# Expert attention of a gated mixture layer: four score slots and a two-tile delay, carried across query blocks, in place of two slots and a one-tile delay

## The chip, the cores and the metric

The kernel runs on all 8 cores of one Trainium2 chip. Each core works on its own batch element and shares nothing with the others but the chip. The metric is device time in microseconds (us) of the slowest core, for one launch.

## What is computed

For each batch element (4096 rows of 1024 values) the reference normalizes the rows, runs a 16-head attention `s`, runs a routed single-head attention `ffn` with 8 experts, and returns `x + s * silu(ffn)`. The change touches only the single-head attention inside `ffn`:

```python
q = jnp.einsum('tc,ecd,te->td', x, q_proj, m)      # D = 128, m is the routing mask
k = jnp.einsum('tc,ecd,te->td', x, k_proj, m)
v = jnp.einsum('tc,ecd,te->td', x, v_proj, m)
scores = jnp.einsum('bqd,bkd->bqk', qh, kh) / jnp.sqrt(D)
scores = jnp.where(causal, scores, jnp.finfo(scores.dtype).min)
attn = jax.nn.softmax(scores, axis=-1)
attn_out = jnp.einsum('bqk,bkd->bqd', attn, vh).reshape(b * t, D)
final = jnp.einsum('td,edc,te->tc', attn_out, o_proj, m * routing_weights)
```

## The kernel before

The kernel is written out by hand: every engine has its own program, and semaphores join them. It runs in stages. First the rows are normalized and transposed and the routing logits computed (up to about 220 us of the span). Then q, k and v of the routed attention are projected, 32 row tiles long (to 568 us). Then comes the stage that the change touches, the causal attention with one head of width 128, from 568.3 to about 710 us. After it the output projection with its Silu writes `g_sp` (to about 895 us), and the 16-head attention and the final combination take the rest, about 2,650 us.

The touched stage works on 8 query blocks `j` of 512 queries. Block `j` sees T = 4j + 4 key tiles `t` of 128 keys, 144 tiles in all; the running number of a tile is g = `c2_g(j, t)`. For every tile four engines take part:

- TensorE computes the scores of 128 keys by 512 queries with one matmul (L721, semaphore `tSf`). Its result goes to one of two slots, the two halves of `PB[0]` (each half is one bank of 512 fp32), by `g % 2`.
- ScalarE takes the exponential of the 512 scores in PSUM and writes them as bf16 to one of two slots of `expC` (L1315, semaphore `aEf`).
- GpSimd takes part in the last four tiles of a block only, which lie on the diagonal: `affine_select` (L481, semaphore `gMf`) zeroes the upper triangle of one 128 x 128 piece and writes it to `maskedf`.
- TensorE multiplies the exponentials, as stationary operand, with the values: up to four matmuls of 129 columns (L707, in `pv_f`), one for each 128 queries, into the four quarters of `PB[1]`. They accumulate over the block, and the 129th column is the sum of the exponentials. The last of each query tile raises `tUf`.

When a block is complete, VectorE reads `PB[1]`: four reciprocals (L1093), then for each query tile a scaling of the routing weights (L1097) and a copy of the sums to SBUF (L1100), and then the drain at L1102 raises `vUf`. GpSimd waits for `vUf` of the block before as well, before it writes the first mask of a block.

TensorE's order is fixed by `tensor_p1`. Within a block it is S(t), PV(t-1), S(t+1), PV(t), where S is the scores and PV are the four matmuls of `pv_f`. S(g) waits until exponential g-2 is done, since it overwrites that slot, and PV(g) waits for exponential g. At the end of the block PV of the last tile is issued by itself, and ahead of the first S of the next block TensorE waits for `vUf`. `expC` is 2048 elements wide, of which two slots of 512 are used in this stage. `PB[2]` is free in this stage: the value projection used it before, and all its readers have finished.

Of the kernel before, what the change touches and what calls it, by code (L numbers as in the profile page):

```python
# [19 lines left out]
def c2_g(j, t):  # L20
    return 2 * j * j + 2 * j + t
# [181 lines left out]
class Builder:  # L203
# [245 lines left out]
    def gpsimd_prog(self, e):  # L449
        s, d, sem = self, self.d, self.sem  # L450
        bar = sem["bar"]
        e.memset(s.onesb[:], 1.0)
        e.drain()
        e.affine_select(s.idt_bf[:], s.onesb[:], [[1, 128]], ALU.is_equal, 0.0,
                        base=0, channel_multiplier=-1)
        e.drain()
        e.engine_nop().then_inc(sem["gInit"], 1)
        if "P0" in self.stages:
            pmap = {0: d["qp"], 1: d["kp"], 2: d["vp"]}
            R3f = [s.R3[:, 0:8192].bitcast(F32)[:, 0:1024],  # L460
                   s.R3[:, 0:8192].bitcast(F32)[:, 1024:2048]]
            for idx in range(24):
                w = pmap[idx // 8]
                a = idx % 8
                if idx >= 2:
                    e.wait_ge(sem["vPc"], idx - 1)
                e.dma_start(R3f[idx % 2],
                            w.rearrange("ee (a p) dd -> p a ee dd", p=128)
                            [:, a:a + 1, :, :]).then_inc(sem["dP0" if idx % 2 == 0 else "dP1"], 16)
        e.drain()  # L470
        e.sem_inc(bar, 1)
        e.wait_ge(bar, 5)
        if "P1" in self.stages:
            for j in range(8):
                if j >= 1:
                    e.wait_ge(sem["vUf"], j * 4)
                for qt in range(4):
                    t = 4 * j + qt
                    g = c2_g(j, t)
                    e.wait_ge(sem["aEf"], g + 1)  # L480
                    e.affine_select(  # L481
                        s.maskedf[:, qt * 128:qt * 128 + 128],
                        s.expC[:, (g % 2) * 512 + qt * 128:(g % 2) * 512 + qt * 128 + 128],
                        [[1, 128]], ALU.is_ge, 0.0,
                        base=0, channel_multiplier=-1).then_inc(sem["gMf"], 1)
            e.wait_ge(sem["sCv"], 8 * NT)
            for c in range(4):
                if c >= 2:
                    e.wait_ge(sem["vOpc"], c - 1)
                e.dma_start(s.stage[:, (c % 2) * 2048:(c % 2) * 2048 + 2048]  # L490
                            .rearrange("p (ee cc) -> p ee cc", ee=2),
                            d["op"].rearrange("ee p cc -> p ee cc")[:, 2 * c:2 * c + 2, :]
                            ).then_inc(sem["dOp0" if c % 2 == 0 else "dOp1"], 16)
        e.drain()
        e.sem_inc(bar, 1)
        e.wait_ge(bar, 10)
        if "P3" in self.stages:
            for p in range(NPAIR):
                for it in P3_PAIRS[p]:
                    if it["kind"] != "C2":  # L500
                        continue
                    j, t = it["j"], it["t"]
                    if t >= 4 * j:
                        qt = t - 4 * j
                        es = it["eslot"]
                        e.wait_ge(sem["aC2"], it["aC2"])
                        for h in range(2):
                            prevu = p * 64 + (6 - j) * 8 + qt * 2 + h + 1
                            if prevu >= 1:
                                e.wait_ge(sem["tU2"], prevu)  # L510
                            e.affine_select(  # L511
                                s.mask2[:, h * 512 + qt * 128: h * 512 + qt * 128 + 128],
                                s.expCs(es)[:, h * 512 + qt * 128:
                                            h * 512 + qt * 128 + 128],
                                [[1, 128]], ALU.is_ge, 0.0,
                                base=0, channel_multiplier=-1).then_inc(sem["gC2"], 1)
                    if t == 4 * j + 3:
                        e.wait_ge(sem["vC2"], p * 64 + (8 - j) * 8)
                        e.dma_start(
                            self.d["s_sp"].rearrange(  # L520
                                "(jj qt p2) (pr h dd) -> p2 jj qt pr h dd",
                                p2=128, jj=8, pr=8, h=2)[:, j, :, p, :, :],
                            s.s_stage[:, (j % 2) * 512:(j % 2) * 512 + 512]
                            .rearrange("p (qt h dd) -> p qt h dd", qt=4, h=2)
                        ).then_inc(sem["dS30" if j % 2 == 0 else "dS31"], 16)
                        if p == NPAIR - 1 and "CMB" in self.stages:
                            self.gpsimd_cmb_q(e, j)
        e.drain()
        e.sem_inc(bar, 1)
        e.wait_ge(bar, 15)  # L530
# [120 lines left out]
    def tensor_p1(self, e):  # L651
        s, sem = self, self.sem
        PB, PBb = s.PB, s.PBb
# [37 lines left out]
        e.wait_ge(sem["sCq"], 8 * NT)  # L691
        e.wait_ge(sem["sCv"], 8 * NT)

        def pv_f(j, t):
            g = c2_g(j, t)
            e.wait_ge(sem["aEf"], g + 1)
            for qt in range(4):
                qtile = 4 * j + qt
                if t > qtile:
                    continue  # L700
                first = (t == 0 and qt in (0, 2))
                if t == qtile:
                    e.wait_ge(sem["gMf"], j * 4 + qt + 1)
                    stat = s.maskedf[:, qt * 128:qt * 128 + 128]
                else:
                    stat = s.expC[:, (g % 2) * 512 + qt * 128:(g % 2) * 512 + qt * 128 + 128]
                mm = e.matmul(PB[1][:, qt * 256:qt * 256 + 129],  # L707
                              stat, vfa[:, t * 130:t * 130 + 129],
                              start=first, stop=(t == qtile), skip_group_check=True)
                if t == qtile:  # L710
                    mm.then_inc(sem["tUf"], 1)

        for j in range(8):
            if j >= 1:
                e.wait_ge(sem["vUf"], j * 4)
            T = 4 * j + 4
            for t in range(T):
                g = c2_g(j, t)
                if g >= 2:
                    e.wait_ge(sem["aEf"], g - 1)  # L720
                e.matmul(PB[0][:, (g % 2) * 512:(g % 2) * 512 + 512],  # L721
                         kfT[:, t * 128:(t + 1) * 128],
                         qfT[:, j * 512:(j + 1) * 512],
                         start=True, stop=True).then_inc(sem["tSf"], 1)
                if t >= 1:
                    pv_f(j, t - 1)
            pv_f(j, T - 1)
        op_r = s.R2[:, 0:8192]
        aoT = [s.Vau[:, 0:1024], s.Vau[:, 1024:2048]]
        e.wait_ge(sem["vOpc"], 4)  # L730
# [539 lines left out]
    def scalar_prog(self, e):  # L1270
        s, sem = self, self.sem
        bar = sem["bar"]
        PB, PBb = s.PB, s.PBb
# [35 lines left out]
        if "P1" in self.stages:  # L1309
            for j in range(8):  # L1310
                T = 4 * j + 4
                for t in range(T):
                    g = c2_g(j, t)
                    e.wait_ge(sem["tSf"], g + 1)
                    e.activation(s.expC[:, (g % 2) * 512:(g % 2) * 512 + 512],  # L1315
                                 PB[0][:, (g % 2) * 512:(g % 2) * 512 + 512],
                                 AF.Exp).then_inc(sem["aEf"], 1)
            for qt in range(NT):
                e.wait_ge(sem["tO4"], qt + 1)
                if qt >= 2:  # L1320
                    e.wait_ge(sem["dG0" if qt % 2 == 0 else "dG1"], 16 * (qt // 2))
                pbo = PB[0] if qt % 2 == 0 else PB[1]
                e.activation(s.gbuf[:, (qt % 2) * 1024:(qt % 2) * 1024 + 1024],
                             pbo[:, :], AF.Silu).then_inc(sem["aS4"], 1)
# [60 lines left out]
```

## Time and profile before

| | us |
|---|---|
| median of 3 runs | 3620.0 |
| lowest and highest | 3560.6 and 3641.5 |
| the profiled execution | 3562.5 |
| its span, slowest core (5) | 3560.9 |
| touched stage on core 5, first score to last PV | 568.3 to 707.8 |

The profile was taken from one execution. Times inside it are counted from the first instruction of core 5, and its span is 1.6 us short of the time of that execution. The median of the runs is 57.5 us above the profiled one. In the timeline, a row gives the start, the time to the end of the (merged) instructions, the engine, the line, and in brackets the idle time of the engine ahead of it with what ended that. Matmuls are pipelined: the duration of one reaches to the modelled arrival of its results, so that the distance from start to start tells more of TensorE's rate.

### The profile page before, as it was taken

The numbers are of one execution on the slowest core, as the hardware profiler recorded it, in microseconds if no ns is written. First come the engines' busy times: TensorE is split into PE (matmuls) and PEld (weight loads), VectorE is DVE, ScalarE is ACT, GpSimd is POOL, SyncE is SP. The second block draws the span as 40 slices with busy tenths as digits, with TensorE's granted clock in tenths as the row PEclk, the third lists the DMA queues.
The fourth block names the chain that finished last, engine by engine and source line by source line (L and its number), as shares of the span: only waits on it lengthen the run. The fifth ranks groups of instructions, "written<-read, shape, count | busy, mean of one in ns | idle before, by whom it ended". The sixth has DMA issues, their size and how long they took to land.

```text
span 3560.9 us, 59880 instructions; the slowest of 8 cores (3533.6 to 3560.9 us)
## 1 busy us (share of the span) xinstructions
PE 2572.6 (72%) x18642; PEld 1157.4 (33%) x18642; DVE 2273.7 (64%) x5890; ACT 2125.0 (60%) x2466; POOL 254.3 (7%) x706
## 2 busy tenths in 40 slices
PE   2179997667377778877777877777787877776551
PEld 1134443333133333333333333333333333332220
DVE  7447773033356776676677667667766766776665
ACT  0000003612057896797788779779877977997762
POOL 0100000000000010010001001000100100011012
PEclk9999997889788768777886886787687578765655
DMA  5410000011400000000000000000000000003346
GB/s 153 139 40 1 1 1 1 12 75 51 159 1 4 4 7 3 4 6 4 4 4 7 3 4 6 6 2 4 7 3 4 7 4 3 6 6 106 113 145 205
DMA packets 35776, 117.11 MB, mean 33 GB/s; under 512 B 5778, under 2 KB 5778, under 8 KB 35474
## 3 DMA queue, kind: packets, MB, share of 16 engines
q1 hardware_dynamic: 22738, 71.34, 6.0%
q0 software_dynamic: 12736, 41.95, 4.1%
q8 instruction: 163, 2.67, 0.3%
q14 instruction: 139, 1.14, 0.1%
HBM read 79.72 MB, written 33.55 MB: 32 GB/s over the span
## 4 chain that ended last, share of the span: by engine, by line
PE 33%; ACT 20%; DVE 18%; issue 15%; DMA 8%; DVEq 4%; POOL 1%; ACTq 0%; SPq 0%; POOLq 0%
ACT expC L1335 7%; ACT stagef L1350 6%; PE PB L881 6%; PE PB L895 5%; PE PB L866 5%; DVE cacc L1075 4%; PE PB L795 4%; PE PB L798 4%; PE PB L810 3%; PE PB L753 3%; ACT stagef L1335 3%; ACT R L1350 3%; DMA stagef<-x 2%; DVE tmpc L1199 2%; DVE stagef L1075 2%
## 5 line engine op out<-in xcount | busy, mean ns | idle before, releaser
L1199 DVE TENSOR_REDUCE tmpc<-stagef 128x2 f32<-128x1024 bf16 (+2 forms) x726 | 811.2, 1127 | 236.0 <-ACT stagef L1350 179.4
L1335 ACT ACTIVATE expC<-PB 128x1024 bf16<-128x1024 f32 x768 | 854.3, 1112 | 87.2 <-PE PB L881 87.2
L1350 ACT ACTIVATE stagef<-PB 128x1024 bf16<-128x1024 f32 x600 | 668.6, 1114 | 208.9 <-PE PB L895 133.6
L1199 DVE TENSOR_REDUCE tmpc<-R 128x2 f32<-128x1024 bf16 (+2 forms) x362 | 406.1, 1122 | 118.2 <-ACT R L1350 89.8
L1335 ACT ACTIVATE stagef<-PB 128x1024 bf16<-128x1024 f32 x384 | 429.7, 1119 | 73.8 <-PE PB L881 73.8
L881 PE MATMUL PB<-R 64*128 64x512 bf16 x1152 | 299.0, 507 | 234.6 <-ACT stagef L1350 138.1
L881 PE MATMUL PB<-QTt,KTt 64*128 64x512 bf16 x1152 | 283.3, 480 | 148.7 <-ACT stagef L1350 80.8
L1350 ACT ACTIVATE R<-PB 128x1024 bf16<-128x1024 f32 x296 | 330.4, 1116 | 81.8 <-PE PB L895 60.1
L681 PE MATMUL PB<-R,xnT 128*128 128x512 bf16 x1536 | 338.9, 381 | 1.0 <-DVE lnat L992 0.9
L1315 ACT ACTIVATE expC<-PB 128x512 bf16<-128x512 f32 x144 | 84.7, 597 | 397.0 <-PE PB L721 391.5
L895 PE MATMUL PB<-R 64*128 64x512 bf16 (+3 forms) x1088 | 264.1, 478 | 37.8 <-ACT expC L1335 20.1
L895 PE MATMUL PB<-KTt,QTt 64*128 64x512 bf16 (+3 forms) x1088 | 250.2, 451 | 47.9 <-ACT expC L1335 27.0
L795 PE MATMUL PB<-xnT,R 128*128 128x512 bf16 x512 | 218.4, 426 | 52.6 <-DVE R L1144 50.2
L798 PE MATMUL PB<-xnT,R 128*128 128x512 bf16 x512 | 214.7, 419 | 0.0
L681 PEld LDWEIGHTS PB<-R,xnT 128*128 128x128 bf16 x1536 | 146.7, 98 | 181.8 <-issue 17.0
L881 PEld LDWEIGHTS PB<-R 64*128 64x128 bf16 x1152 | 72.9, 98 | 390.9 <-issue 386.6
L866 PE MATMUL PB<-R,expC 128*128 128x65 bf16 x2680 | 186.2, 223 | 15.3 <-DVEq L1267 15.3
L866 PE MATMUL PB<-Vau,expC 128*128 128x65 bf16 x2680 | 178.6, 218 | 14.6 <-DVEq L1267 14.6
L866 PEld LDWEIGHTS PB<-R,expC 128*128 128x128 bf16 x2680 | 134.8, 115 | 135.1 <-issue 135.1
L866 PEld LDWEIGHTS PB<-Vau,expC 128*128 128x128 bf16 x2680 | 128.7, 111 | 126.9 <-issue 126.9
L881 PEld LDWEIGHTS PB<-QTt,KTt 64*128 64x128 bf16 x1152 | 72.0, 97 | 293.1 <-issue 289.0
L511 POOL TENSOR_SCALAR_AFFINE_SELECT mask<-expC 128x128 bf16<-128x128 bf16 x304 | 81.2, 290 | 1201.0 <-ACT expC L1335 1122.8
(162 smaller groups left out, 2973.5 us busy)
## 6 DMA issues: line engine op xcount, KB each, us to landing
stagef<-x SPq DMA_DIRECT2D x64, 512.0 KB, 4.5
out<-Vau SPq DMA_DIRECT2D x32, 512.0 KB, 3.6
g_sp<-stagef SPq DMA_DIRECT2D x32, 256.0 KB, 2.1
s_sp<-s_stage POOLq DMA_DIRECT2D x64, 128.0 KB, 2.4
QTt<-g_sp POOLq DMA_DIRECT2D x32, 256.0 KB, 5.7
KTt<-s_sp POOLq DMA_DIRECT2D x32, 256.0 KB, 5.9
R<-qp POOLq DMA_DIRECT2D x8, 512.0 KB, 5.4
R<-kp POOLq DMA_DIRECT2D x8, 512.0 KB, 4.7
```

Source lines behind the costliest of these rows:

```text
L681: last = e.matmul(PB[pb][:, half * 512:(half + 1) * 512], s.xnT[:, ct * 4096 + qt * 128: ct * 4096 + (qt + 1) * 128], src[:, ct * 1024 + h ...
L753: last = e.matmul(pbo[:, half * 512:(half + 1) * 512], aoT[qt % 2][:, ei * 128:(ei + 1) * 128], op_r[:, ei * 1024 + half * 512: ei * 1024 ...
L795: e.matmul(POOL[it["slot"]][:, 0:512], Wq[:, ct * 1024 + pp * 128: ct * 1024 + (pp + 1) * 128], mv, start=(ct == 0), stop=(ct == 7), skip_ ...
L798: last = e.matmul(POOL[it["slot"]][:, 512:1024], Wk[:, ct * 1024 + pp * 128: ct * 1024 + (pp + 1) * 128], mv, start=(ct == 0), stop=(ct == 7),
L810: last = e.matmul(POOL[it["slot"]][:, 0:512], Wv[:, ct * 1024 + pp * 128: ct * 1024 + (pp + 1) * 128], mv, start=(ct == 0), stop=(ct == 7) ...
L866: e.matmul(PB[2][:, h * 512 + qt * 128: h * 512 + qt * 128 + 65], stat, Vau[:, t * 130 + h * 65: t * 130 + h * 65 + 65], start=first, stop ...
L881: last = e.matmul(POOL[it["slot"]][:, h * 512:h * 512 + 512], stat, mv, start=True, stop=True, tile_position=(64 * h, 0))
L895: last = e.matmul(POOL[it["slot"]][:, h * 512:h * 512 + kw], statq, mvk, start=True, stop=True, tile_position=(64 * h, 0))
L1075: e.scalar_tensor_tensor(out, PB[pb][:, ei * 128:(ei + 1) * 128], mask[:, qt * 8 + ei:qt * 8 + ei + 1], acc[:], ALU.mult, ALU.add).then_in ...
L1199: e.tensor_reduce(s.tmpc[:].rearrange("p (h c) -> p h c", h=2)[:, :, c:c + 1], s.c1scr((m1 - 1) % 3)[:, 0:2 * kw] .rearrange("p (h k) -> p ...
L1335: e.activation(s.expCs(es), PB[[0, 1, 3][it["slot"]]][:, :], AF.Exp).then_inc(sem["aC2"], 1)
L1350: e.activation(scr[:, 0:1024], pbsrc[:, 0:1024], AF.Exp).then_inc(sem["aC1"], 1)
```

## The change

Scores get four slots instead of two: the halves of `PB[0]` and those of `PB[2]`. `expC` gets four slots too, which it has room for. TensorE keeps a list of pending tiles and issues PV two tiles behind the scores, S(g), PV(g-2), and the list runs on over the ends of the blocks: the last two PV of a block are issued after the first two or three S of the next. S(g) now waits for exponential g-4. The wait for `vUf` moves from ahead of the first S of a block to ahead of the first PV of a block, which is the first instruction that overwrites `PB[1]`. ScalarE and GpSimd read and write the slots by `g % 4`. The number of matmuls, exponentials, masks and VectorE operations, and their shapes, stay the same.

```diff
@@ gpsimd_prog
-                        s.expC[:, (g % 2) * 512 + qt * 128:(g % 2) * 512 + qt * 128 + 128],
+                        s.expC[:, (g % 4) * 512 + qt * 128:(g % 4) * 512 + qt * 128 + 128],
@@ tensor_p1
+        SCF = [PB[0][:, 0:512], PB[0][:, 512:1024],
+               PB[2][:, 0:512], PB[2][:, 512:1024]]
+
         def pv_f(j, t):
             g = c2_g(j, t)
             e.wait_ge(sem["aEf"], g + 1)
+            if t == 0 and j >= 1:
+                e.wait_ge(sem["vUf"], j * 4)
...
-                    stat = s.expC[:, (g % 2) * 512 + qt * 128:(g % 2) * 512 + qt * 128 + 128]
+                    stat = s.expC[:, (g % 4) * 512 + qt * 128:(g % 4) * 512 + qt * 128 + 128]
...
+        pendf = []
         for j in range(8):
-            if j >= 1:
-                e.wait_ge(sem["vUf"], j * 4)
             T = 4 * j + 4
             for t in range(T):
                 g = c2_g(j, t)
-                if g >= 2:
-                    e.wait_ge(sem["aEf"], g - 1)
-                e.matmul(PB[0][:, (g % 2) * 512:(g % 2) * 512 + 512],
+                if g >= 4:
+                    e.wait_ge(sem["aEf"], g - 3)
+                e.matmul(SCF[g % 4],
                          kfT[:, t * 128:(t + 1) * 128],
                          qfT[:, j * 512:(j + 1) * 512],
                          start=True, stop=True).then_inc(sem["tSf"], 1)
-                if t >= 1:
-                    pv_f(j, t - 1)
-            pv_f(j, T - 1)
+                if len(pendf) >= 2:
+                    pv_f(*pendf.pop(0))
+                pendf.append((j, t))
+        for pv in pendf:
+            pv_f(*pv)
@@ scalar_prog
-                    e.activation(s.expC[:, (g % 2) * 512:(g % 2) * 512 + 512],
-                                 PB[0][:, (g % 2) * 512:(g % 2) * 512 + 512],
+                    pbf = PB[0] if (g % 4) < 2 else PB[2]
+                    e.activation(s.expC[:, (g % 4) * 512:(g % 4) * 512 + 512],
+                                 pbf[:, (g % 2) * 512:(g % 2) * 512 + 512],
                                  AF.Exp).then_inc(sem["aEf"], 1)
```

## Rows read from the trace of the kernel before

**Rows 1.** Busy time of each engine by stretch, core 5; start:end length, busy..., PEclk, DMA
```profile
core 5: us, PE busy (x) PEld busy (x) DVE busy (x) ACT busy (x) POOL busy (x), PEclk, DMA share, GB/s
568.30:707.80 139.50, 97.85 (x672) 47.16 (x672) 12.47 (x84) 84.66 (x144) 9.50 (x33) 0.82 0.00 1
900.00:3560.00 2660.00, 1947.03 (x15232) 857.45 (x15232) 1797.94 (x4440) 1991.20 (x2241) 220.08 (x640) 0.73 0.09 28
```

**Rows 2.** Groups of instructions in the touched stage: busy, mean ns, idle before
```profile
L1315 ACT ACTIVATE expC<-PB 128x512 bf16<-128x512 f32 x144 | 84.7, 597 | 397.0 <-PE PB L721 391.5
```

**Rows 3.** Timeline in the middle of block 3, full clock
```profile
608.24 1.24 ACT L1315 ACTIVATE expC<-PB 128x512 bf16<-128x512 f32 x2 [0.20 <-PE PB L721]
...
608.98 0.39 PE L707 MATMUL PB<-R,expC 128*128 128x129 bf16 x4 [0.20 <-ACT expC L1315]
609.20 0.38 PE L721 MATMUL PB<-R 128*128 128x512 bf16 x1
...
609.68 1.24 ACT L1315 ACTIVATE expC<-PB 128x512 bf16<-128x512 f32 x2 [0.21 <-PE PB L721]
```

**Rows 4.** Timeline after the start of block 3, half clock
```profile
602.00 0.60 ACT L1315 ACTIVATE expC<-PB 128x512 bf16<-128x512 f32 x1 [0.77 <-PE PB L721]
602.13 0.63 PE L721 MATMUL PB<-R 128*128 128x512 bf16 x1
602.74 0.59 PE L707 MATMUL PB<-R,expC 128*128 128x129 bf16 x4
...
603.13 0.63 PE L721 MATMUL PB<-R 128*128 128x512 bf16 x1
...
603.86 2.73 ACT L1315 ACTIVATE expC<-PB 128x512 bf16<-128x512 f32 x4 [0.40 <-PE PB L721]
603.99 0.47 PE L721 MATMUL PB<-R 128*128 128x512 bf16 x1
```

**Rows 5.** Timeline from the diagonal of block 3 into block 4
```profile
610.84 0.22 PE L707 MATMUL PB<-R,mask 128*128 128x129 bf16 x1 [0.62 <-POOL mask L481]
...
611.54 1.18 ACT L1315 ACTIVATE expC<-PB 128x512 bf16<-128x512 f32 x2 [0.63 <-PE PB L721]
...
613.28 0.22 PE L707 MATMUL PB<-R,mask 128*128 128x129 bf16 x1 [0.31 <-POOL mask L481]
613.61 0.36 DVE L1093 RECIPROCAL dinv<-PB 128x1 f32<-128x1 f32 x4 [14.43 <-PE PB L707]
...
616.43 1.08 ACT L1315 ACTIVATE expC<-PB 128x512 bf16<-128x512 f32 x2 [3.71 <-PE PB L721]
```

**Rows 6.** The first two scores of the eight blocks, TensorE's timeline
```profile
568.31 1.01 PE L721 MATMUL PB<-R 128*128 128x512 bf16 x2 [3.70 <-DVE R L1088]
575.70 1.01 PE L721 MATMUL PB<-R 128*128 128x512 bf16 x2 [2.25 <-DVEq L1102]
586.21 1.01 PE L721 MATMUL PB<-R 128*128 128x512 bf16 x2 [2.25 <-DVEq L1102]
599.46 1.01 PE L721 MATMUL PB<-R 128*128 128x512 bf16 x2 [2.25 <-DVEq L1102]
615.75 1.01 PE L721 MATMUL PB<-R 128*128 128x512 bf16 x2 [2.25 <-DVEq L1102]
635.13 1.01 PE L721 MATMUL PB<-R 128*128 128x512 bf16 x2 [2.25 <-DVEq L1102]
657.61 1.01 PE L721 MATMUL PB<-R 128*128 128x512 bf16 x2 [2.25 <-DVEq L1102]
682.54 0.92 PE L721 MATMUL PB<-R 128*128 128x512 bf16 x2 [2.25 <-DVEq L1102]
```

**Rows 7.** Exponentials of 1024 columns back to back, 16-head stage
```profile
1518.67 1.07 ACT L1350 ACTIVATE R<-PB 128x1024 bf16<-128x1024 f32 x1
1519.58 1.08 ACT L1335 ACTIVATE expC<-PB 128x1024 bf16<-128x1024 f32 x1
```

**Rows 8.** Span and mean granted clock, fastest and slowest core
```profile
core 2: 3533.6 us, clock 0.793
...
core 5: 3560.9 us, clock 0.787
```

## What was predicted

> **What bounds the kernel now.** I first read the busy time by stretch [rows 1]. The stage of the change lasts 139.5 us, and in it ScalarE is busy 84.7 us and TensorE 97.9 us by its modelled durations. No engine is full there, and the mean granted clock is 0.82. The stages behind it start only when it has ended, so a microsecond saved in it is one saved at the end, unless a later stage gives it back. The whole stage is 3.9% of the span, which caps anything the change can do.
>
> Then I asked what each engine waits for. ScalarE's 144 exponentials of 0.597 us [rows 2] wait for scores. The timeline shows why [rows 3]: this is a loop of latencies, not an engine at its limit. An exponential starts at 608.24 and lasts 0.60, 0.14 us later (608.98) PV of that tile starts, 0.22 us later (609.20) the next score matmul is issued behind it, and 0.48 us later (609.68) its exponential starts. That is 1.44 us for a round, and with two tiles in flight 0.72 us a tile.
>
> The same loop at TensorE's lower clock (1.2 GHz; a score matmul lasts 0.63 us instead of 0.38) takes 0.60 + 0.14 + 0.39 + 0.73 = 1.86 us, 0.93 a tile [rows 4].
>
> The third part is the end of a block [rows 5]. In block 3 the last exponential ends at 611.54 + 1.18 = 612.72 (call it E), the last PV at 613.50 (E + 0.78), VectorE reads out, and TensorE may go on at 615.75 [rows 6], E + 3.03. ScalarE idles 3.71 us. All seven block ends show the same 2.25 us of idle TensorE, and behind every one the first two scores take about 1.01 us together, which is the lower clock (at the last, 0.92, the clock rises early) [rows 6]. It comes back about 4.5 us later: block 3 starts at 599.46 and its score at 603.99 is down to 0.47 us [rows 4].
>
> **The change, part by part.** No instruction is added or dropped; everything is in the order and the waits.
>
> *Three tiles in flight.* PV(g) is now followed by S(g+3). The round of 1.44 us carries three tiles, 0.48 us a tile. Two other limits lie at the same place, and I work both out. ScalarE: exponentials whose inputs are ready start 1.08 - 0.60 = 0.48 us apart (the first pair of a block, [rows 5]), and those of 1024 columns 0.91 us apart [rows 7], well under their length of 1.07. TensorE at full clock: PV takes 0.22 us from its start to the next S, and S streams 512 columns at 2.4 GHz, 0.21 us, so about 0.44 us. With three limits between 0.44 and 0.48 some slips are likely, and I take 0.50 us a tile. The bounds are 0.48 and 0.60, the latter if exponentials did not overlap at all.
>
> *The same at 1.2 GHz.* The loop would allow 1.86 / 3 = 0.62 us, but TensorE itself needs 0.39 for PV [rows 4] and 512 / 1.2 = 0.43 for S, together about 0.82; score to score after score was 0.86 at 603.13 to 603.99, and I take 0.86. Here the gain is small, since TensorE becomes the bound.
>
> *The block end.* S of the next block no longer waits for VectorE. Three scores of the next block are issued before TensorE stops at the first PV, which waits for `vUf`. They cost no time: their exponentials (3 x 0.48 = 1.44 us) fill ScalarE while VectorE reads out. The readout stays as late as before, E + 3.03, because the last PV still needs the last exponential and its mask. Queued behind the waiting PV is S of the fourth tile, and ScalarE waits for that one: a stall moves, it doesn't vanish. From the release (call it R) the fourth exponential starts after 0.39 + 0.73 = 1.12 us at the lower clock [rows 4]. I assume that the clock still falls: TensorE still stands for about 2 us.
>
> *Masks.* On the diagonal PV starts later after its exponential: 610.84 against 609.68 + 0.60 = 610.28 is 0.56 us [rows 3, 5], 0.42 more than the 0.14 within a block. With the PV of the first diagonal tile feeding the score of the last tile, this appears once in a block, 0.42 us. GpSimd is not at its limit: 9.5 us busy in the stage [rows 1].
>
> **The sum.** From release to release a block of T tiles takes 1.12 (fourth exponential) + 4 x 0.86 = 3.44 (lower clock, until about R + 4.56) + (T - 8) x 0.50 + 0.42 (mask) + 0.60 (last exponential) + 3.03 = 8.61 + 0.50 (T - 8). For T = 8 the mask hides under the slower tiles: 8.19. Against the distances of the block starts [rows 6]:
>
> - block 1: 8.2 for 10.5, saves 2.3
> - block 2: 10.6 for 13.3, saves 2.6
> - block 3: 12.6 for 16.3, saves 3.7
> - block 4: 14.6 for 19.4, saves 4.8
> - block 5: 16.6 for 22.5, saves 5.9
> - block 6: 18.6 for 24.9, saves 6.3
> - block 7, to its last PV (E + 0.78): 20.6 - 2.25 = 18.4 for 682.54 to about 707.76, 25.2, saves 6.9
> - block 0, four diagonal tiles: one score less in its chain, an estimated 0.7
>
> Together 33 us, of which 84 tiles x 0.22 = 18.5 come from the loop at full clock and the rest from the block ends. The stage would take about 106 us. The load of the output projection's weights starts when the last mask is issued, and all behind it moves forward whole. 3562.5 - 33 = 3529 us for an execution like the profiled one. The median of the runs shown is 57.5 us above it; the same saving from there gives 3587.
>
> On ScalarE's rate the Trainium skill ("ScalarE: Activation LUTs", What ACT_TABLE_LOAD costs) says that an ACTIVATE with immediate scale and bias takes 186 ns + 0.833 ns an element, and that back-to-back ones overlap by about 93 ns. That would be 613 - 93 = 520 ns for 512 elements, an estimate from the page; the row of the block's first pair says 0.48. By the page the 84 full-clock tiles would cost 1.7 us more than at 0.50, and the saving would be 31 us.
>
> **The rivals.**
>
> *ScalarE is the bound sooner.* In today's loop the second of a pair starts 1.24 - 0.60 = 0.64 us after the first [rows 3]. If that is ScalarE's own pace when a semaphore is checked, and not the wait for scores, the 84 tiles take 0.64: 84 x 0.14 = 11.8 us less saved, 21 us, 3541. Against it: the pair at 0.48 has the same waits in it.
>
> *The clock doesn't fall at the block ends.* TensorE has one more score in the gap and is denser ahead of it. Then each of seven blocks saves 4 x (0.86 - 0.50) + (1.12 - 0.70) = 1.86 us more, 13 us: 46 saved, 3516. Against it: the fall stands at all seven gaps of 2.25 us, and the new gaps are about as long.
>
> *The clock stays down for whole blocks.* Then 84 x 0.36 = 30 us are lost again, 3 us remain, 3559. Against it: in every block from 1 on the clock rose with less work on TensorE than it would have now.
>
> *Slower, by the later stages' clock.* The 16-head stage runs at a mean of 0.73 [rows 1], and a core that differs by 0.006 in clock over the run differs by 27 us [rows 8]. If the denser stage, or merely the shifted start, left the later clock lower by 0.008, the 33 us would be gone, and by about 0.024 (33 + 71 us) the kernel would be slower by 2%. For it: nothing but that spread between equal programs. Against it: the stage ends some 190 us and one whole stage before that part.
>
> **How the numbers follow.** The forecast has a chance of 0.62 (its own range 3520 to 3540 around 3529), ScalarE at 0.64 has 0.10, the clock kept up 0.13, the clock kept down 0.08, slower 0.07 (0.03 of it over 2%). The point is that of the forecast. The range goes from 3505, the kept clock with another 11 us for the differences between cores, to 3605: the runs of before lie up to 79 us above the profiled one, and the same shift of a median execution ends at 3587. A measurement of this kernel can tell about 2%, 71 us, from no change. For faster by 71 us the stage would have to halve, while its exponentials alone take 144 x 0.48 = 69 us of 139; I give 0.07 for the later stages adding to it. Within 2%: 0.90. Slower: 0.03.
>
> **What would show it.** Right: exponentials about 0.48 to 0.50 us apart in the middle of blocks 3 to 7; ScalarE's idle time at a block end down from 3.7 to about 2 us, ended by a score behind the PV that waits for VectorE; score matmuls of 0.63 us just behind R; the stage's stretch 106 us long with ScalarE busy still near 85; the later stages as long as before. Wrong: exponentials at 0.6 or more at full clock (ScalarE or the loop), no score of 0.63 us after block ends (clock kept), PV more than 0.22 us apart from S with no wait, which would mean that weight loads are no longer hidden, or a 16-head stage that changes by more than 20 us.

## The result

| | before | changed |
|---|---|---|
| median of the runs, us | 3565.9 (10 runs, 3554.1 to 3641.5) | 3511.5 (9 runs, 3509.1 to 3601.7) |
| profiled execution, us | 3562.5 | 3520.2 |
| its span, slowest core | 3560.9 (core 5) | 3518.4 (core 1) |
| touched stage, first score to end of last PV, mean of the cores | 139.1 | 95.7 |

The changed kernel takes 0.9861 of the time of the kernel before, 95% interval 0.9836 to 0.9885, which is 50 us less (41 to 58). The ratio leaves out those executions of either kernel that ran about 2% slow, with the cores of a die at a lower granted clock, while the medians above include them. The gain is under 2%, but its interval is clear of no change. Timed a second time beside other kernels the changed kernel took 0.9878 (0.9860 to 0.9895), 43 us less. That is the 43 us by which the touched stage shrank in both profiles (95.7 us each time), so I take 43 as the gain. The first interval reaches down to 41, and what its 50 us hold beyond 43 isn't explained; it may be scatter.

The busy time by stretch of the changed kernel, its slowest core, has the same columns as [rows 1]: start:end, length, then busy time and number of instructions for each engine, granted clock, share of DMA.

```profile
core 1: us, PE busy (x) PEld busy (x) DVE busy (x) ACT busy (x) POOL busy (x), PEclk, DMA share, GB/s
569.30:666.40 97.10, 78.63 (x672) 46.18 (x672) 12.48 (x84) 74.49 (x144) 9.45 (x33) 0.91 0.00 1
...
860.00:3518.00 2658.00, 1937.85 (x15232) 854.70 (x15232) 1797.65 (x4440) 1991.21 (x2241) 221.13 (x640) 0.74 0.09 28
```

The stage is 97 us long where it was 139.5 [rows 1], with the same 672 matmuls and 144 exponentials. The mean granted clock in it rose from 0.82 to 0.91. Behind the stage nothing changed: from its end to the end of the run this core takes 3518.4 - 666.4 = 2,852.0 us, core 5 before took 3560.9 - 707.8 = 2,853.1, and the mean granted clock of the long stretch behind is 0.74 beside 0.73.

ScalarE's timeline over blocks 2 and 3 (start, time to the end of the merged instructions, idle time before with its releaser) shows what has become of [rows 3 to 5]:

```profile
583.09 4.03 ACT L1322 ACTIVATE expC<-PB 128x512 bf16<-128x512 f32 x8 [1.86 <-PE PB L725]
587.40 1.57 ACT L1322 ACTIVATE expC<-PB 128x512 bf16<-128x512 f32 x3 [0.28 <-PE PB L725]
589.16 0.60 ACT L1322 ACTIVATE expC<-PB 128x512 bf16<-128x512 f32 x1 [0.19 <-PE PB L725]
592.03 0.60 ACT L1322 ACTIVATE expC<-PB 128x512 bf16<-128x512 f32 x1 [2.28 <-PE PB L725]
592.89 0.60 ACT L1322 ACTIVATE expC<-PB 128x512 bf16<-128x512 f32 x1 [0.26 <-PE PB L725]
593.75 0.60 ACT L1322 ACTIVATE expC<-PB 128x512 bf16<-128x512 f32 x1 [0.26 <-PE PB L725]
594.56 4.51 ACT L1322 ACTIVATE expC<-PB 128x512 bf16<-128x512 f32 x9 [0.21 <-PE PB L725]
599.36 1.08 ACT L1322 ACTIVATE expC<-PB 128x512 bf16<-128x512 f32 x2 [0.28 <-PE PB L725]
```

Eight exponentials in 4.03 us are (4.03 - 0.60) / 7 = 0.49 us apart, where they were 0.72. At a block end ScalarE idles 1.86 us where the clock is kept and up to 2.28 us where it fell, where it idled 3.71 us before, and three exponentials of the next block (the last two of the x3 group and the single one behind it) come ahead of that gap. The 0.28 us inside each block is a wait for the mask: 0.60 + 0.28 - 0.49 = 0.39 us lost once. The 0.19 us two tiles later is a second one; here it costs nothing, since the fourth exponential of the next block waits for the readout anyway.

The same kernel's timeline of all engines at the end of block 3, into block 4:

```profile
600.52 0.22 PE L712 MATMUL PB<-R,mask 128*128 128x129 bf16 x1 [0.31 <-ACT expC L1322]
600.65 0.38 PE L725 MATMUL PB<-R 128*128 128x512 bf16 x1
600.85 0.36 DVE L1099 RECIPROCAL dinv<-PB 128x1 f32<-128x1 f32 x4 [10.11 <-PE PB L712]
601.12 0.60 ACT L1322 ACTIVATE expC<-PB 128x512 bf16<-128x512 f32 x1 [0.18 <-PE PB L725]
...
602.88 0.39 PE L712 MATMUL PB<-R,expC 128*128 128x129 bf16 x4 [1.85 <-DVEq L1108]
603.11 0.38 PE L725 MATMUL PB<-R 128*128 128x512 bf16 x1
...
603.58 5.00 ACT L1322 ACTIVATE expC<-PB 128x512 bf16<-128x512 f32 x10 [1.86 <-PE PB L725]
```

The last PV of block 3 starts at 600.52, behind the second score of block 4, the third score follows, and TensorE waits 1.85 us for VectorE's readout. Then PV and the fourth score are issued, and ScalarE's wait ends 0.70 us behind the release. Matmuls are still at 0.39 and 0.38 us: the clock was kept over this gap. At the end of block 2 on the same core it was not:

```profile
590.92 0.59 PE L712 MATMUL PB<-R,expC 128*128 128x129 bf16 x4 [1.86 <-DVEq L1108]
591.30 0.63 PE L725 MATMUL PB<-R 128*128 128x512 bf16 x1
...
592.16 0.63 PE L725 MATMUL PB<-R 128*128 128x512 bf16 x1
...
593.88 0.58 PE L725 MATMUL PB<-R 128*128 128x512 bf16 x1
...
594.53 0.38 PE L725 MATMUL PB<-R 128*128 128x512 bf16 x1
```

The granted clock of the same core says the same: 0.50 (1.2 GHz) behind the end of block 2 and 1.00 (2.4 GHz) behind that of block 3, in the columns of [rows 1].

```profile
591.00:594.00 3.00, 3.00 (x20) 2.17 (x20) 0.00 (x0) 1.44 (x3) 0.00 (x0) 0.50 0.00 0
603.00:606.00 3.00, 3.00 (x34) 1.93 (x33) 0.00 (x0) 2.42 (x5) 0.00 (x0) 1.00 0.00 0
```

### The profile page after: what moved, and what is told of

It reads as the page before. It is cut to its first block, busy times and chain, and to the rows that moved or that the text cites. A ratio compares the mean times of both kernels' runs of the same rounds, so it can differ in the third digit from the quotient of the medians.

```text
span 3518.4 us, 59878 instructions; the slowest of 8 cores (3491.2 to 3518.4 us)
## 1 busy us (share of the span) xinstructions
PE 2544.7 (72%) x18642; PEld 1153.6 (33%) x18642; DVE 2273.6 (65%) x5890; ACT 2114.8 (60%) x2466; POOL 255.4 (7%) x706
## 4 chain that ended last, share of the span: by engine, by line
PE 32%; ACT 22%; DVE 18%; issue 15%; DMA 8%; DVEq 4%; POOL 0%; ACTq 0%; SPq 0%; POOLq 0%
ACT expC L1342 7%; ACT stagef L1357 6%; PE PB L887 6%; PE PB L901 5%; PE PB L872 5%; DVE cacc L1081 4%; PE PB L801 4%; PE PB L804 4%; PE PB L759 3%; ACT stagef L1342 3%; PE PB L816 3%; ACT R L1357 3%; DMA stagef<-x 3%; DVE tmpc L1205 2%; DVE stagef L1081 2%
## 5 line engine op out<-in xcount | busy, mean ns | idle before, releaser
L1322 ACT ACTIVATE expC<-PB 128x512 bf16<-128x512 f32 x144 | 74.5, 610 | 364.8 <-PE PB L725 364.8
L887 PEld LDWEIGHTS PB<-R 64*128 64x128 bf16 x1152 | 72.9, 98 | 392.3 <-issue 388.4
```

The source lines that it names most:

```text
L887: last = e.matmul(POOL[it["slot"]][:, h * 512:h * 512 + 512], stat, mv, start=True, stop=True, tile_position=(64 * h, 0))
```

## The experiments

All kernels keep the rest of the program. The edits are shown against the changed kernel, except for e1 (against e3) and e8 (against the kernel before). The stage is measured in each profile from the first score to the end of the last PV, on every core; a score at half clock is one whose record is over 0.45 us (0.63 at the lower clock, 0.38 at the full one). Where a kernel was timed in rounds, the ratio is to the kernel before on the same chip.

| kernel | stage, mean (range) us | scores at half clock, mean of a core | ratio, 95% interval |
|---|---|---|---|
| before | 139.1 (138.1 to 140.6) | 40.4 | 1 |
| changed | 95.7 (92.5 to 100.1) | 18.5 | 0.9861 (0.9836 to 0.9885) |
| changed, again | 95.7 (92.6 to 97.2) | 19.1 | 0.9878 (0.9860 to 0.9895) |
| e3_slots_only | 138.9 (138.2 to 139.3) | 38.8 | |
| e2_carry_only | 129.4 (129.1 to 130.2) | 36.8 | 0.9975 (0.9964 to 0.9987) |
| e1_lag2_drained | 111.0 (110.0 to 112.0) | 42.2 | 0.9935 (0.9916 to 0.9955) |
| e4_lag3_carried | 87.3 (85.0 to 89.6) | 13.8 | |
| e5_filler | 91.5 (91.2 to 91.7) | 6.6 | |
| e8_before_filler | 132.6 (131.9 to 136.0) | 3.8 | |
| e6_two_acc | 78.0 (77.7 to 78.4) | 6.9 | 0.9825 (0.9811 to 0.9839) |
| e7_two_acc_lag3 | 73.2 (72.9 to 73.3) | 7.6 | 0.9866 (0.9800 to 0.9931) |
| e9, the same again | 73.2 (72.9 to 73.3) | 7.1 | 0.9815 (0.9798 to 0.9832) |

(On two of the eight cores 12 or 13 of the 144 records of scores are missing in each profile, so the counts of half-clock scores are a little low for all kernels. The other six have all of them. The kernels without a ratio ran once, for their profile.)

### The parts of the change, one at a time

**Four slots alone.** The order of the kernel before, with four slots:

```diff
-            if t == 0 and j >= 1:
-                e.wait_ge(sem["vUf"], j * 4)
...
         for j in range(8):
+            if j >= 1:
+                e.wait_ge(sem["vUf"], j * 4)
             T = 4 * j + 4
...
-                if len(pendf) >= 2:
+                if len(pendf) >= 1:
                     pv_f(*pendf.pop(0))
                 pendf.append((j, t))
-        for pv in pendf:
-            pv_f(*pv)
+            while pendf:
+                pv_f(*pendf.pop(0))
```

> Four slots, but the order of the kernel before: PV one tile behind, drained at block ends, wait for VectorE ahead of the first score. Theory: TensorE's order and not the slots holds the loop, since a score is issued behind the PV that waits; nothing changes, 0.72 us a tile, stage 139 us. Rival (the slots held it): tiles under 0.6 us apart, stage under 125 us.

The stage took 138.9 us, as the kernel before. The timeline (core 3) at the end of a block is the old one, with a pair of exponentials 1.25 - 0.60 = 0.65 us apart and 3.71 us of idle ScalarE:

```profile
607.90 1.25 ACT L1322 ACTIVATE expC<-PB 128x512 bf16<-128x512 f32 x2 [0.19 <-PE PB L725]
...
614.69 1.08 ACT L1322 ACTIVATE expC<-PB 128x512 bf16<-128x512 f32 x2 [3.71 <-PE PB L725]
```

So more slots alone don't speed up the loop: what held it is the place of the score in TensorE's order, behind a PV that waits. The slots are a condition of the longer delay, since three tiles in flight need three of them.

**Two tiles behind, drained at the block ends.** As e3, but with the delay of the changed kernel; against e3 the diff is

```diff
-                if len(pendf) >= 1:
+                if len(pendf) >= 2:
```

> Four slots and PV two tiles behind the scores, but drained at the end of each block, with the wait for VectorE ahead of the first score as in the kernel before. Theory (a loop of 1.44 us shared by three tiles instead of two): exponentials 0.49 us apart in the middle of a block, ScalarE idle 3.7 us at block ends as before, the clock low after all seven; the touched stage about 139.5 - 84 x 0.23 - 6 = 114 us, the kernel about 25 us under the kernel before. Rival (most of the gain is the wait moved past the block end): stage above 125 us, gain under 12 us.

The stage took 111.0 us, 28 us less than before, and the kernel 23 us less (16 to 30). ScalarE and TensorE around a block start, core 1:

```profile
607.72 0.81 PE L725 MATMUL PB<-R 128*128 128x512 bf16 x3 [2.24 <-DVEq L1108]
608.19 1.57 ACT L1322 ACTIVATE expC<-PB 128x512 bf16<-128x512 f32 x3 [3.50 <-PE PB L725]
608.93 0.51 PE L710 MATMUL PB<-R,expC 128*128 128x129 bf16 x4 [0.41 <-ACT expC L1322]
609.23 0.63 PE L725 MATMUL PB<-R 128*128 128x512 bf16 x1
...
612.54 4.05 ACT L1322 ACTIVATE expC<-PB 128x512 bf16<-128x512 f32 x8 [0.26 <-PE PB L725]
```

The last row gives (4.05 - 0.60) / 7 = 0.49 us a tile, with the old stall of 3.5 us in place. At this block start the clock is still up for three scores and falls a little later; over the stage the scores at half clock are about as many as before (42.2 and 40.4 a core). The loop is the larger part of the change, as the theory said, and the rival (most of it at the block ends) falls.

**Carried over the block end, one tile behind, two slots.**

```diff
-                if g >= 4:
-                    e.wait_ge(sem["aEf"], g - 3)
-                e.matmul(SCF[g % 4],
+                if g >= 2:
+                    e.wait_ge(sem["aEf"], g - 1)
+                e.matmul(SCF[g % 2],
...
-                if len(pendf) >= 2:
+                if len(pendf) >= 1:
```

with `g % 2` for all slots of `expC`.

> Two slots and PV one tile behind as in the kernel before, but the pending tile is carried over the block end and the wait for VectorE stands ahead of the first PV. Theory: still 0.72 us a tile inside a block; each block end gives about 1.4 us (the third exponential of a block at E + 4.15 us instead of E + 5.56 us), 10 us in all, stage about 129 us; more by up to 13 us if the clock stays up over the shorter gaps. Rival (most of the gain is here): stage under 110 us.

129.4 us against about 129 expected, and the kernel 9 us faster (5 to 13). Core 2:

```profile
612.90 0.59 PE L712 MATMUL PB<-R,expC 128*128 128x129 bf16 x4 [1.85 <-DVEq L1108]
613.28 0.63 PE L725 MATMUL PB<-R 128*128 128x512 bf16 x1
...
614.01 0.60 ACT L1322 ACTIVATE expC<-PB 128x512 bf16<-128x512 f32 x1 [2.27 <-PE PB L725]
```

The gap of TensorE is 1.85 us, as in the changed kernel, and the clock is down behind it. On the six cores with all 144 score records every block of this kernel has scores at half clock behind its gap.

The two parts give 28.1 + 9.7 = 37.8 us, the whole change 43.4. The 5.6 us more are not in either part.

### Where the missing part is: the clock

**The gap filled with matmuls.** Eight matmuls of score size go to the unused `PB[3]` ahead of the wait for VectorE. Their result is never read; the output is computed as before.

```diff
             if t == 0 and j >= 1:
+                for _ in range(8):
+                    e.matmul(PB[3][:, 0:512], kfT[:, 0:128], qfT[:, 0:512],
+                             start=True, stop=True)
                 e.wait_ge(sem["vUf"], j * 4)
```

> The changed kernel with eight score-sized matmuls into the unused PB[3] just ahead of the wait for VectorE at each of the seven block ends; their result is never read. They take 8 x 0.216 = 1.73 us, inside the 1.86 us that TensorE stands idle. Theory (whether the clock falls at a block end decides the difference between blocks of equal length): no score matmul above 0.45 us behind a block end, all blocks at the length of the best ones of the changed kernel (8.5, 10.5, 12.5, 14.4, 16.4 us for blocks 2 to 6), stage about 91 us on every core instead of 91 to 100. Rival (the differences come from something else, such as semaphore timing): lengths stay mixed.

The stage is 91.2 to 91.7 us on all eight cores, where the changed kernel spreads from 92.5 to 100.1. Behind its first block end no score is at half clock on any of the six cores with complete records (the half-clock scores left are those of block 0 and two or three of block 1 that come ahead of the gap). Block 3 on core 5 (all engines):

```profile
588.00 1.89 PE L702 MATMUL PB<-R 128*128 128x512 bf16 x8
...
590.01 0.39 PE L715 MATMUL PB<-R,expC 128*128 128x129 bf16 x4
590.24 0.38 PE L728 MATMUL PB<-R 128*128 128x512 bf16 x1
```

The fillers end at 589.89, VectorE releases PV at 590.01, and the next score is at full clock. ScalarE still idles 1.86 us, so nothing but the clock differs. The changed kernel has 11.9 more half-clock scores a core, and its stage is 4.2 us longer: 0.35 us each, close to the 0.86 - 0.49 = 0.37 between the two paces.

**The same in the kernel before** (the diff is against it), with nine of them, ahead of the wait at the block start:

```diff
             if j >= 1:
+                for _ in range(9):
+                    e.matmul(PB[3][:, 0:512], kfT[:, 0:128], qfT[:, 0:512],
+                             start=True, stop=True)
                 e.wait_ge(sem["vUf"], j * 4)
```

> The kernel before with nine score-sized matmuls into the unused PB[3] ahead of the wait for VectorE at each block end; their result is never read. 9 x 0.216 = 1.94 us, inside the 2.25 us of idle TensorE. Theory: the clock stays up, the exponentials of a block come at 0.72 us from the start instead of 0.9, about 1.2 us saved a block end, stage about 130 instead of 139 us. If the clock still falls in the rest of the gap or was no part of it: 139 us.

132.6 us, 6.5 us under the kernel before (9 expected); only block 0 has scores at half clock on the six cores with complete records. Core 5, the start of block 1 (the first two rows) and of block 3:

```profile
572.51 3.67 PE L716 MATMUL PB<-R 128*128 128x512 bf16 x9
576.49 1.08 ACT L1318 ACTIVATE expC<-PB 128x512 bf16<-128x512 f32 x2 [4.61 <-PE PB L724]
...
612.66 0.59 PE L724 MATMUL PB<-R 128*128 128x512 bf16 x2 [0.31 <-DVEq L1105]
613.14 1.09 ACT L1318 ACTIVATE expC<-PB 128x512 bf16<-128x512 f32 x2 [3.50 <-PE PB L724]
...
614.58 1.09 ACT L1318 ACTIVATE expC<-PB 128x512 bf16<-128x512 f32 x2 [0.35 <-PE PB L724]
```

The pairs come 1.44 us apart from the first tile on. At the end of block 0 the fillers themselves start at half clock, take 3.67 us and outlast the readout, so that ScalarE idles 4.61 us and not 3.5. That happens there on every core (4.25 to 4.83 us) and at three more block ends on core 2, which is its 136.0 us: about 1.6 us in the mean of the cores. Without this delay the gain would be about 8 us, an estimate near the expected 9, and the count says the same: 36.6 fewer half-clock scores at 0.93 - 0.72 = 0.21 us each make 7.7.

So the low clock behind the block ends cost about 8 us in the kernel before (6.5 of them gained by e8) and 4.2 us still in the changed one. On the six cores with complete records the clock fell behind 22 of the 42 gaps of the changed kernel, in its first profile and in the second. In the first profile it was kept into blocks 1, 2 and 4 on five of these cores each, into block 3 on none, into block 5 on one and into blocks 6 and 7 on two each; in the second it was kept into blocks 1 to 7 on three, three, none, six, none, four and four. Core 5 of the first profile kept it nowhere, and its stage is the longest, 100.1 us. In the kernel before, in e1 (the same dense blocks with the longer gap, 2.24 us) and in e2 (the short gap of 1.85 us with the looser blocks) it was kept over none.

Blocks of equal length give the price of a fall: block 6 takes 17.8 us from release to release where the clock fell and 16.4 where it was kept, block 4 takes 13.7 and 12.5, block 2 takes 10.0 and 8.5. That is 1.2 to 1.5 us a fall. With 3.3 of 7 gaps kept on a core, some 4 to 5 of the 5.6 us that neither part has are the clock's, an estimate from these blocks.

### What holds the new pace

**PV three tiles behind.**

```diff
-                if len(pendf) >= 2:
+                if len(pendf) >= 3:
```

> The changed kernel with PV three tiles behind instead of two. Theory (at 0.49 us a tile ScalarE is at its own pace, 0.48): the pace stays 0.49 although the loop would now allow 0.36; each block end gains one exponential, ScalarE's idle time 1.86 to about 1.4 us, 7 x 0.48 = 3.4 us, stage about 94 us. Rival (the loop still binds at 0.48): the pace falls to TensorE's 0.44 and the stage to about 88 us.

The stage took 87.3 us, not 94, and ScalarE's idle time at a block end is 1.66 us, not 1.4. The pace itself did not change. All engines of core 1, behind the start of block 5, and under it ScalarE's own timeline there:

```profile
613.71 0.38 PE L725 MATMUL PB<-R 128*128 128x512 bf16 x1
...
614.15 0.38 PE L725 MATMUL PB<-R 128*128 128x512 bf16 x1
...
614.59 0.38 PE L725 MATMUL PB<-R 128*128 128x512 bf16 x1
```

```profile
613.22 9.45 ACT L1322 ACTIVATE expC<-PB 128x512 bf16<-128x512 f32 x19 [0.26 <-PE PB L725]
```

TensorE catches up here with scores 0.44 us apart, which is its own pace; ScalarE takes 9.45 us for 19 exponentials, (9.45 - 0.60) / 18 = 0.49. So the loop and TensorE are free to go faster and ScalarE isn't. The 8.4 us add up from three places: 7 x 0.48 = 3.4 from one more exponential in each gap (expected), 8 x 0.39 = 3.1 from the mask wait, which is gone inside the blocks and which I had left out, and the rest, about 1.9, fits the 4.7 fewer half-clock scores (4.7 x 0.37 = 1.7). The clock fell behind 10 of the 42 gaps of six cores here, with the gaps at 1.85 us as in the changed kernel.

**Two accumulators.** Even blocks accumulate in `PB[1]`, odd ones in `PB[3]`, so that no PV waits for the readout just ahead of it:

```diff
-            if t == 0 and j >= 1:
-                e.wait_ge(sem["vUf"], j * 4)
+            if t == 0 and j >= 2:
+                e.wait_ge(sem["vUf"], (j - 1) * 4)
+            acc = PB[1] if j % 2 == 0 else PB[3]
...
-                mm = e.matmul(PB[1][:, qt * 256:qt * 256 + 129],
+                mm = e.matmul(acc[:, qt * 256:qt * 256 + 129],
```

and `vector_p1` reads the same one.

> The changed kernel with two accumulators, PB[1] for even and PB[3] for odd blocks, so that the first PV of a block waits for the readout of the block before the last. Theory (what is left at a block end is TensorE's wait for VectorE's readout): no idle time above 0.4 us on ScalarE inside the stage, stage about 144 x 0.49 + 8 x 0.3 + 2 = 75 us, the kernel about 19 us under the changed kernel, 0.5%. Rival (the readout then gets in the way elsewhere, for example of the masks, which wait for the same semaphore): a stage above 85 us.

ScalarE's timeline, core 1:

```profile
591.64 1.57 ACT L1324 ACTIVATE expC<-PB 128x512 bf16<-128x512 f32 x3 [0.28 <-PE PB L726]
593.40 8.43 ACT L1324 ACTIVATE expC<-PB 128x512 bf16<-128x512 f32 x17 [0.18 <-PE PB L726]
602.12 1.57 ACT L1324 ACTIVATE expC<-PB 128x512 bf16<-128x512 f32 x3 [0.29 <-PE PB L726]
603.88 10.40 ACT L1324 ACTIVATE expC<-PB 128x512 bf16<-128x512 f32 x21 [0.19 <-PE PB L726]
```

Only the two short waits for the masks are left, 0.28 and 0.18 us a block, which set the next start back by 0.39 and 0.29 us. The stage takes 78.0 us (75 expected; I had counted one wait, and at 0.3 us), the kernel 0.9825 of the kernel before, 62 us less.

**Both.** Two accumulators and PV three tiles behind:

> Two accumulators and PV three tiles behind. Theory: ScalarE never waits, also not on the diagonal, stage about 144 x 0.49 + 2 = 73 us, 2 us under the one with two tiles. Rival (ScalarE is not at its own pace at 0.49): stage under 68 us, TensorE's 144 x 0.44 + 2.

ScalarE's timeline, core 5, the whole stage from its fourth group on, and the busy time of the stage:

```profile
574.75 64.79 ACT L1324 ACTIVATE expC<-PB 128x512 bf16<-128x512 f32 x132 [0.23 <-PE PB L726]
```

```profile
core 5: us, PE busy (x) PEld busy (x) DVE busy (x) ACT busy (x) POOL busy (x), PEclk, DMA share, GB/s
567.20:640.30 73.10, 70.14 (x672) 43.23 (x672) 12.47 (x84) 71.07 (x144) 9.39 (x33) 0.97 0.01 2
```

132 exponentials run without a gap, (64.79 - 0.60) / 131 = 0.49 us apart, and ScalarE is busy 71.1 of 73.1 us. The stage is at ScalarE's limit. The first timing of this kernel had a wide interval, so it was timed again, together with the changed kernel:

> The same kernel as e7_two_acc_lag3, timed again, since its first interval was wide. If the time follows the touched stage (73.2 us there, 139.1 in the kernel before): 66 us under the kernel before, ratio 0.9815. If later stages give part back: above 0.985.

> The changed kernel unaltered, timed on the same chip as e9. Its stage is 43 us shorter than before (mean of the cores), its first ratio 0.9861 says 50 us. If the later stages are unchanged: ratio 0.988. If they gain as well: 0.986 again.

0.9815 (0.9798 to 0.9832) of the kernel before, 66 us less, as the stage says; the changed kernel came to 0.9878, the 43 us of its stage. This version beats both kernels.

## Why the prediction was right, and where it was off

The forecast was 3529 us with 33 us saved, in a range of 3505 to 3605. The median came to 3511.5 and the saving to 43 us in the stage, so sign, place and mechanism hold and the size was a quarter too small. The median lies inside the stated range, but below the 3520 to 3540 that the forecast itself was given, and nearer to the rival's 3516; the profiled execution, 3520.2, is at that edge. The prediction also said that a measurement can tell about 2% from no change. The intervals here are 0.2% to 0.3% wide on either side, and 1.2% stood clear.

**The loop: right.** 1.44 us shared by three tiles, 0.50 us a tile taken, 0.49 measured, in the changed kernel and in e1, where it stands alone. The sum's 18.5 us for the full-clock tiles became 84 x 0.23 = 19.3. That ScalarE sets it, and not the loop or TensorE, was left open by the prediction (three limits between 0.44 and 0.48); e4 and e7 show ScalarE. The rival with 0.64 us is refuted. One sign was read wrong: ScalarE's busy time was to stay near 85 us and came to 74.5, since records of 0.60 us that start 0.49 apart overlap and busy time counts the overlap once. The estimate from the Trainium skill ("ScalarE: Activation LUTs", What ACT_TABLE_LOAD costs), 0.52 us, is not what is measured: (64.79 - 0.60) / 131 = 0.49 in e7, and the measurement decides.

**The stall moves and shrinks: right.** ScalarE's idle time went from 3.71 to 1.86 us at full clock (predicted "about 2"), ended by the score behind the PV that waits for VectorE. From the release the fourth exponential took 0.70 and 1.11 us at the two clocks, predicted 0.70 and 1.12. The release came 602.88 - (599.36 + 0.60) = 2.92 us after the last exponential instead of 3.03, 0.7 us over the blocks. The mask cost 0.39 once a block, predicted 0.42.

**The clock: the step that was mis-sized.** The prediction put the half clock behind all seven block ends, 7 x 1.86 = 13 us, with the sentence "I assume that the clock still falls: TensorE still stands for about 2 us". Measured is 4.2 us (the changed kernel against e5, where it falls behind no block end). That is 8.8 us of the roughly 10.5 us by which the stage (106 predicted, 95.7 measured) was shorter. Both factors were too large: the clock fell behind about half of the ends, and a fall cost 1.2 to 1.5 us, since about three steps from tile to tile and not four are 0.86 us behind it (592.03, 592.89, 593.75, 594.56 in the timeline above). Core 5, where it fell behind all seven, still took only 100.1 us. The blocks of core 1 show it one by one, from release to release (the column before is core 5 of the kernel before, as in the prediction):

| block | before | predicted | measured | half-clock scores behind its release |
|---|---|---|---|---|
| 1 | 10.5 | 8.2 | 6.6 | 0 |
| 2 | 13.3 | 10.6 | 8.5 | 0 |
| 3 | 16.3 | 12.6 | 12.0 | 4 |
| 4 | 19.4 | 14.6 | 12.5 | 0 |
| 5 | 22.5 | 16.6 | 15.6 | 3 |
| 6 | 24.9 | 18.6 | 17.8 | 4 |
| 7 | 25.2 | 18.4 | 17.7 | 4 |

Where the clock fell (blocks 3, 5, 6, 7) the formula is off by 0.6 to 1.0 us, and where it was kept by 1.6 (block 1) and 2.1 (2 and 4). The pace of 0.49 makes 0.8 us of the sum, the earlier release 0.7, and together with the clock about 10.3 us, nearly all of the difference.

The evidence of the kernel before, seven gaps out of seven, was taken as evidence on the gap alone. But the change altered two things at once, the length of the gap (2.25 to 1.85 us) and how densely TensorE works ahead of it. e1 and e2 change one each and keep the clock nowhere; both together keep it at about half of the ends. At nearly the same gap of 1.85 us the falls go from 42 of 42 (e2) to 22 (changed) to 10 (e4) as the blocks get denser. The rival "the clock doesn't fall at the block ends" was given too small a chance, 0.13: the truth lies between it and the forecast. Its price, 46 us saved, agrees with the 47.6 of e5 partly by luck, as 13 us for the clock was too much and the 33 us under it too little. Why one block end keeps the clock and another doesn't isn't settled.

**Slower, by the later stages: nothing of it.** The mean time from the end of the stage to the end of the run over the cores is 2,840 us, 2,843 before. It is 2,849 in the profile of e1, 6 us more than before, so of the 28 us of its stage about 22 are left at the end, and it was timed at 23 us less.

## What to carry to other kernels

When no engine is full, look for a round of latencies and count the tiles that share it: here 1.44 us over two tiles became 1.44 over three, and adding buffers without changing the order of the in-order engine gained nothing (138.9 for 139.1 us). Carry the software pipeline over the ends of blocks, and put the wait for a readout ahead of the first instruction that overwrites what is read; if a spare accumulator is to be had, the wait goes away altogether, which gave another 18 us of the 96. Price the clock of TensorE as a term of its own, and when a change both shortens a gap and fills the work around it, keep both outcomes in the forecast.

## What the runs showed of the hardware

- TensorE's clock fell behind every gap of 2.25 us in the kernel before and of about 1.85 us in e2, but behind only 22 of the 42 gaps of 1.85 us in the changed kernel, whose blocks are denser, and 10 of 42 in e4. A fall cost 1.2 to 1.5 us in the changed kernel. Matmuls whose result nobody reads, put into the gap, kept the clock up at all of them and saved 4.2 us of 95.7 (6.5 of 139.1 in the kernel before, where at some ends they ran at half clock themselves and outlasted the wait).
- Exponentials of 512 columns from PSUM come 0.49 us apart, 132 in a row, with single records of 0.60 us. In that stream the mean record grows to 0.81 us: a record's duration says nothing of the pace once instructions queue.

```profile
L1324 ACT ACTIVATE expC<-PB 128x512 bf16<-128x512 f32 x144 | 71.1, 807 | 344.2 <-PE PB L726 344.2
```

(e7, core 5, the groups of the stage: busy us, mean ns, idle before.) The busy time of the group, 71.1 us, divided by 144 gives the pace, 0.49.
